# A graph kernel in which the counts of edges are built for 16 targets at a time instead of 32

## The chip, the cores and the metric

One Trainium2 chip, one of its cores. The metric is the device time of one execution in microseconds; the lower the better.

## The reference

1024 nodes with 128 features, 32768 edges sorted by their target, 64 features an edge. Two graph layers are computed:

```python
h = maximum(layernorm(x), 0)                       # [1024, 128]
m = mlp3(concat(h[src], h[dst], edge_attr))        # 320 -> 256 -> 256 -> 128, per edge
summed = segment_sum(m, src) + segment_sum(m, dst) # [1024, 128]
x = x + mlp3(concat(h, summed, attention(h)))      # attention: differences of paired blocks of 32 nodes
h = maximum(layernorm(x), 0)
deg = 1 + number of edges with this target
out = segment_sum over edges and self loops of dinv[src] * dinv[dst] * (h @ W)[src]  + b,  dinv = 1/sqrt(deg)
x = x + gelu(out)
```

The second layer needs, for every pair of nodes, how many edges lead from one to the other. The kernel builds this 1024 x 1024 table of counts while the edges of the first layer pass, and multiplies with it at the end.

## The kernel before, in words

**Head.** Layer norm, transposes, and two tables in DRAM (`table_a`, `table_b`) that hold each node's share of the first edge layer for source and target. GpSimd gathers rows of them by indirect DMA, 8 gathers for a group of 4 tiles of 128 edges (L446, L454), 64 groups in all, three buffers. VectorE prepares the edge indices, finds for each window of targets the first tile in which it occurs (L1156 to L1179) and writes it to `rows_i` (L1202).

**The loop over groups.** Each engine has a list of its own for group g, run by `run_groups`, unrolled:

- TensorE (`group`, L677): second layer of g (L607, 12 products of 512 columns), first layer of g+1 (L587, 4 products, then 8 transposes L593 that add the gathered rows), the scatter of tile 0 of g-1 between the two halves of that first layer, messages of g (L617), the scatter of tiles 1 to 3 of g-1 (L628). The count products (L646) stand one behind each of five transposes.
- ScalarE (`group`, L827): rounds the edges (L825), relu of both layers (L796, L802), the distance of each node's number to the middle of an edge's two ends (L812), rounds the messages (L819), and after every second group copies a window of counts out of PSUM (L853).
- VectorE (`group`, L1008): in this order one-hots of the next window (two pairs), incidence row 1 of g-1 (L1005), the sum of the gathered rows of g+1 (L1048, two halves), a pair of one-hots, incidence 2, low part of the edges of g+2 (L979), low part of the first layer (L985), incidence 3, one-hots, the other low part, one-hots, incidence 0 of g, low part of the messages (L991), and after every second group the sums of a window (L1076, L1078).

**The counts.** The sorted edges are cut into 32 windows of 32 targets. A window gets 10 tiles of edges, which covers what it spans. For each tile VectorE writes `oh_low` (128 x 128: which of 128 low source numbers) and `oh_key` (128 x 258, three rows of 86 padded to 88: which target and upper source number, 32 x 8 keys), and TensorE multiplies the two into `bank[2]`. Ten such products make the window (5 in each group). ScalarE copies it into `ct_sb`; VectorE sums it over sources (`into_part`) and targets (`from_part`). Where a window spans more than its tiles, a loop of extra visits adds the rest (`more_windows`); it runs at least once. With these inputs it runs once, both at 10 tiles for 32 targets and at 6 tiles for 16 targets. It stands behind group 62 on VectorE and in group 63 on TensorE. Then come the degrees (L664, L1145) and the bias of the messages times the number of edges (L1151).

**The end.** After the scatter of the last group TensorE adds that bias by 8 transposes (L672), ScalarE and VectorE copy the halves of the sums, and the update network (L714, L720, L728), the second layer norm, the product with the counts (L765), `gcn_W` (L744) and gelu follow.

## Time and profile before

| | us |
|---|---|
| median of 3 runs | 767.13 (765.44 to 767.53) |
| the profiled execution | 765.72 |
| its span | 763.9 |
| TensorE busy | 736.0 (96%) |
| VectorE busy | 729.5 (96%) |
| GpSimd busy | 539.0 (71%) |
| ScalarE busy | 524.3 (69%) |

The rows further down are times in us from the start of the span. A timeline row is: start, duration, engine and line, operation, output <- input with shapes, number of instructions merged; in brackets the idle time of the engine before it and what ended it. Ends of matmuls are modelled, and neighbouring instructions of an engine overlap somewhat, so the distance from start to start is what one costs in a row of them.

### The profile page before, as it was taken

How to read it: one execution, taken by the hardware profiler on the slowest of the kernel's cores; microseconds unless marked ns; L12 is line 12 of the kernel's file. 1: busy time of each engine (PE TensorE's matmuls, PEld its weight loads, DVE VectorE, ACT ScalarE, POOL GpSimd, SP SyncE). 2: the span in 40 equal slices, each digit the busy share in tenths (PEclk: the TensorE clock that was granted, in tenths of full speed). 3: DMA queues.
4: the chain of work that ended last, by engine and by line, in shares of the span. 5: the costliest groups of instructions: out<-in, count | busy, mean ns of one | idle time of the engine just before them, and what ended most of it. 6: DMA issues, size and time to landing. Idle time of an engine off the chain costs nothing.

```text
span 763.9 us, 13342 instructions
## 1 busy us (share of the span) xinstructions
PE 736.0 (96%) x4171; PEld 619.3 (81%) x4171; DVE 729.5 (96%) x1506; ACT 524.3 (69%) x711; POOL 539.0 (71%) x533
## 2 busy tenths in 40 slices
PE   7589999999999999999999999999999999999896
PEld 6467888888888888888888888888888888888755
DVE  7889999999999999999999999999999999999775
ACT  3256777777777777777777777777777777776623
POOL 3777777777777777777777777777777777777100
PEclk9899999999999999999999999999999999999999
DMA  7534444344434444344443444434443444432000
GB/s 227 164 119 129 128 127 123 117 126 129 126 112 125 130 128 127 114 124 128 127 124 113 130 129 126 126 112 127 129 126 113 126 127 130 126 111 83 0 1 28
DMA packets 42566, 90.15 MB, mean 118 GB/s; under 512 B 11136, under 2 KB 17920, under 8 KB 42496
## 3 DMA queue, kind: packets, MB, share of 16 engines
q0 software_dynamic: 24576, 67.14, 28.6%
q1 hardware_dynamic: 17920, 22.16, 9.9%
q8 instruction: 33, 0.54, 0.3%
q14 instruction: 37, 0.30, 0.1%
HBM read 86.64 MB, written 2.62 MB: 117 GB/s over the span
## 4 chain that ended last, share of the span: by engine, by line
PE 88%; DVE 4%; POOL 3%; issue 2%; DMA 2%; ACT 1%; DVEq 0%; SPq 0%; POOLq 0%
PE bank L628 30%; PE bank L607 22%; PE bank L617 14%; PE bank L587 7%; PE bank L593 7%; PE bank L646 4%; POOL rows_sb L446 2%; POOL rows_sb L454 1%; DVE ring L1005 1%; PE bank L720 1%; DMA w_sb<-mW 1%; PE bank L765 1%; PE bank L728 1%; DMA table_a<-rows_sb 0%; PE bank L714 0%
## 5 line engine op out<-in xcount | busy, mean ns | idle before, releaser
L446 POOL DMA_INDIRECT rows_sb<-table_a,ends_i x256 | 263.5, 1029 | 82.2 <-issue 77.7
L454 POOL DMA_INDIRECT rows_sb<-table_b,ends_i x256 | 262.7, 1026 | 78.0 <-issue 78.0
L812 ACT ACTIVATE dist<-iota_h,neg_mid 128x1026 f16<-128x1026 f16 (+1 forms) x256 | 292.3, 1143 | 0.0
L1005 DVE TENSOR_SCALAR ring<-dist,half_gap,times 128x1026 fp32r<-128x1026 f16 (+1 forms) x256 | 276.4, 1081 | 1.7 <-ACT dist L812 0.6
L628 PE MATMUL bank<-ring,m_hi 128*128 128x512 f32 x512 | 172.4, 418 | 1.3 <-DVE ring L1005 1.1
L802 ACT ACTIVATE h_sb<-bank,b_sb 128x512 f32<-128x512 f32 x128 | 87.6, 684 | 122.5 <-PE bank L607 122.5
L628 PE MATMUL bank<-ring,m_lo 128*128 128x512 f32 x512 | 160.8, 395 | 0.0
L607 PE MATMUL bank<-ring,w_hi 128*128 128x512 f32 x512 | 150.0, 394 | 1.4 <-DVE ring L985 1.4
L1057 DVE TENSOR_SCALAR oh_key<-iota_h,key_f,minus_base 128x258 bf16<-128x258 f16 x321 | 128.5, 400 | 0.0
L617 PE MATMUL bank<-w_sb,h_sb 128*128 128x128 f32 x1024 | 124.8, 275 | 0.0
L593 PE MATMUL bank<-ident,rows_sb 128*128 128x128 f32 x512 | 113.7, 276 | 8.0 <-DVE rows_sb L1048 8.0
L617 PEld LDWEIGHTS bank<-w_sb,h_sb 128*128 128x128 f32 x1024 | 119.5, 192 | 0.1
L796 ACT ACTIVATE ring<-bank 128x512 fp32r<-128x512 f32 x128 | 76.7, 599 | 60.1 <-PE bank L593 55.8
L607 PEld LDWEIGHTS bank<-ring,w_hi 128*128 128x128 f32 x512 | 96.1, 188 | 24.4 <-DVE ring L985 2.0
L628 PEld LDWEIGHTS bank<-ring,m_lo 128*128 128x128 f32 x512 | 96.9, 189 | 23.2
L628 PEld LDWEIGHTS bank<-ring,m_hi 128*128 128x128 f32 x512 | 87.2, 191 | 13.9 <-DVE ring L1005 2.0
L985 DVE SCALAR_TENSOR_TENSOR ring<-bank,ring 128x512 fp32r<-128x512 f32 x128 | 87.8, 686 | 3.7 <-ACT ring L796 1.7
L593 PEld LDWEIGHTS bank<-ident,rows_sb 128*128 128x128 f32 x512 | 70.3, 142 | 20.7 <-DVE rows_sb L1048 11.2
L1056 DVE TENSOR_SCALAR oh_low<-iota_h,low_f 128x128 bf16<-128x128 f16 x321 | 84.8, 264 | 2.2 <-issue 2.1
L1048 DVE TENSOR_TENSOR rows_sb<-rows_sb 128x512 f32<-128x512 f32 x128 | 82.2, 681 | 3.7 <-DMA rows_sb<-table_b,ends_i 3.6
L607 PE MATMUL bank<-ring,w_lo 128*128 128x512 f32 x256 | 80.3, 395 | 0.0
L646 PE MATMUL bank<-oh_key,oh_low 128*128 128x258 bf16 x320 | 77.8, 275 | 0.0
(182 smaller groups left out, 628.5 us busy)
## 6 DMA issues: line engine op xcount, KB each, us to landing
e_raw<-edge_attr_t SPq DMA_DIRECT2D x128, 128.0 KB, 3.1
rows_sb<-table_a,ends_i POOLq DMA_INDIRECT x256, 2.8
rows_sb<-table_b,ends_i POOLq DMA_INDIRECT x256, 2.9
table_a<-rows_sb SPq DMA_DIRECT2D x4, 256.0 KB, 3.4
table_b<-rows_sb SPq DMA_DIRECT2D x4, 256.0 KB, 2.5
x_sb<-x SPq DMA_DIRECT2D x2, 256.0 KB, 3.2
out<-oh_key SPq DMA_DIRECT2D x4, 128.0 KB, 1.8
u_sb<-uW SPq DMA_DIRECT2D x1, 384.0 KB, 5.0
```

The costliest lines, as they stand in the source:

```text
L446: nc.gpsimd.indirect_dma_start(got[:, b, t, 0, :], None, table_a, bass.IndirectOffsetOnAxis(ap=ends_i[:, 0, tile:tile + 1], axis=0),).then ...
L454: nc.gpsimd.indirect_dma_start(got[:, b, t, 1, :], None, table_b, bass.IndirectOffsetOnAxis(ap=ends_i[:, 1, tile:tile + 1], axis=0),).then ...
L593: mm = nc.tensor.matmul(z1t_bank[k][:, t * P:(t + 1) * P], got[:, g % GB, t, 0, part], ident[:, :], start=False, stop=True, is_transpose=T ...
L607: mm = nc.tensor.matmul(z2_bank[m][:, :], w[:, k, m * P:(m + 1) * P], a[:, b, k, :], start=(n == 0), stop=(n == len(parts) - 1))
L617: mm = nc.tensor.matmul(msg_bank[:, t * D:(t + 1) * D], h2_sb[:, k, t * P:(t + 1) * P], w3_sb[:, k, :], start=(t == 0 and k == 0), stop=(k ...
L628: mm = nc.tensor.matmul(acc_bank[n][:, :], part[:, b, t, :], inc[:, t, n * HB:(n + 1) * HB], start=(is_first(g) and t == 0 and part is m_h ...
L646: mm = nc.tensor.matmul(bank[2][:, 0:KR * KN], oh_low[:, w % HOT, j, :], oh_key[:, w % HOT, j, :, 0:KN], start=(j == 0), stop=(j == VT - 1 ...
L802: nc.scalar.activation(h2_sb[:, m, :], z2_bank[m][:, :], ACT.Relu, bias=b2_sb[:, m:m + 1]).then_inc(h2_ready, 1)
L812: nc.scalar.activation(to, of, ACT.Abs, bias=neg_mid[:, bass.ds(g * GT + t, 1)]).then_inc(dist_ready, 1)
L985: nc.vector.scalar_tensor_tensor(h1_lo[:, b, k, :], z1t_bank[k][:, :], 0.0, h1_hi[:, b, k, :].bitcast(F32), ALU.max, ALU.subtract).then_in ...
L1005: nc.vector.tensor_scalar(to, of, half_gap[:, tile], times[:, tile], ALU.is_equal, ALU.mult).then_inc(inc_ready, 1)
L1057: return nc.vector.tensor_scalar(oh_key[:, slot, j, :, 0:KN], iota_h[:, 0:KR * KN].rearrange("p (r n) -> p r n", r=KR), key_f[:, bass.ds(t ...
```

## The change

- A window is 16 targets wide instead of 32, there are 64 instead of 32, each gets 6 tiles instead of 10. `oh_key` is 128 columns, flat, without padding. One-hots have four buffers instead of two. VectorE makes two windows in each of the groups -1, 0 and 1, and one in each of the groups 2 to 59; window 0 is no longer built before the loop.
- TensorE counts a whole window (6 products in a row) between the first layer of g+1 and the messages of g, no longer one product behind a transpose. Two windows share a half of `bank[2]`.
- ScalarE clears `ct_sb` in the head with 8 activations of scale 0 (six after its table copies, two after its copies of the node part), and no longer copies windows. VectorE adds each pair of windows to `ct_sb` out of PSUM (`pair_out`), waits for that add, and sums as before, once for a pair.
- The extra visits are made ahead of the loop, behind the clears, and no longer touch the sums. `iota_f` moves to the memory of `dist`, since `ct_sb` is cleared.
- The degrees come one group earlier. The bias is added before the scatter of the last group, and that scatter does first all of the first 512 nodes and then the others (`last_scatter`).

```diff
-    VT = 10
-    NW = 32
+    VT = 6
+    NW = 64
     WD = N // NW
     WK = WD * NC
-    KR, KN, KP = 3, 86, 88
+    PAIRS = NW // 2
+    PD = 2 * WD
+    PK = 2 * WK
...
-    HOT = 2
+    HOT = 4
...
-        oh_key = sb("oh_key", [P, HOT, VT, KR, KP], BF16)
+        oh_key = sb("oh_key", [P, HOT, VT, WK], BF16)
...
-        from_part = sb("from_part", [P, NW, NC])
-        add_into = sb("add_into", [P, WD])
-        add_from = sb("add_from", [P, NC])
+        from_part = sb("from_part", [P, PAIRS, NC])
...
-        iota_f = ct_sb[:, 0, :]
+        iota_f = dist[:, :, :].rearrange("p t n -> p (t n)").bitcast(F32)[:, 0:N]
...
-        LAST_W = 2 * (NW - 1)
-
-        def made_in(i):
-
-            return 0 <= i and i + 1 < NW
-
-        def summed_in(b, i):
-
-            return b == 0 and 0 <= i < NW
+        FILL = 2
+
+        def made_in(g):
+
+            if g < FILL:
+                return [2 * (g + 1), 2 * (g + 1) + 1]
+            return [w for w in (g + 2 + FILL,) if w < NW]
+
+        def counted_in(g):
+
+            if 0 <= g <= FILL:
+                return [2 * g, 2 * g + 1]
+            return [w for w in (g + 1 + FILL,) if FILL < g and w < NW]
+
+        def summed_in(g):
+
+            pairs = [p for p in range(PAIRS) if 2 * p + 1 in counted_in(g - 1)]
+            return pairs[0] if pairs else None
+
+        LAST_SUM = NW - 1 - FILL
...
-            def first_layer(g, b, n, k, counting):
+            def first_layer(g, b, n, k):
...
-                    if counting and t in COUNTS_AT[k]:
-                        count_tile(counting[0], counting[1] * (VT // 2) + t - COUNTS_AT[k][0] + k * len(COUNTS_AT[0]))
...
-                return (w, (g + 1) % 2) if 0 <= w < NW else None
-
-            def count_tile(w, j):
-
-                if j % (VT // 2) == 0:
-                    pe.wait_ge(w_hot, 2 * w + j // (VT // 2) + 1)
-                if j == 0:
-                    wait(pe, w_out, w)
-                mm = nc.tensor.matmul(bank[2][:, 0:KR * KN], oh_low[:, w % HOT, j, :], oh_key[:, w % HOT, j, :, 0:KN],
-                                      start=(j == 0), stop=(j == VT - 1), skip_group_check=True)
-                if j == VT - 1:
-                    mm.then_inc(w_psum, 1)
+            def count_window(w):
+
+                pe.wait_ge(w_hot, w + 1)
+                if w % 2 == 0:
+                    wait(pe, w_out, w // 2 - 1)
+                at = (w // 2) % 2 * PK + w % 2 * WK
+                for j in range(VT):
+                    mm = nc.tensor.matmul(bank[2][:, at:at + WK], oh_low[:, w % HOT, j, :], oh_key[:, w % HOT, j, :],
+                                          start=(j == 0), stop=(j == VT - 1), skip_group_check=True)
+                mm.then_inc(w_psum, 1)
...
-                pe.wait_ge(w_out, NW)
                 visits = pe.value_load(rows_i[0:1, 2 * NW - 1:2 * NW], min_val=1, max_val=MORE)
                 with pe.Fori(0, visits) as v:
                     pe.wait_ge(more_hot, v + 1)
-                    nc.tensor.matmul(bank[2][:, 0:KR * KN], oh_low[:, 0, 0, :], oh_key[:, 0, 0, :, 0:KN],
+                    nc.tensor.matmul(bank[2][:, 0:WK], oh_low[:, 0, 0, :], oh_key[:, 0, 0, :],
                                      start=True, stop=True, skip_group_check=True).then_inc(more_psum, 1)
...
-                    mm = nc.tensor.matmul(acc_bank[c // 4][:, (c % 4) * P:(c % 4 + 1) * P], cb3[:, c, :], ident[:, :],
-                                          start=False, stop=(c % 4 == 3), is_transpose=True, skip_group_check=True)
-                    if c % 4 == 3:
-                        mm.then_inc(sums_ready, 1)
+                    nc.tensor.matmul(acc_bank[c // 4][:, (c % 4) * P:(c % 4 + 1) * P], cb3[:, c, :], ident[:, :],
+                                     start=False, stop=False, is_transpose=True, skip_group_check=True)
+
+            def last_scatter(g, b):
+
+                pe.wait_ge(m_lo_ready, g + 1)
+                for n in range(NH):
+                    for t in range(GT):
+                        if n == 0:
+                            pe.wait_ge(inc_ready, GT * g + (t + 1))
+                        for part in (m_hi, m_lo):
+                            mm = nc.tensor.matmul(acc_bank[n][:, :], part[:, b, t, :], inc[:, t, n * HB:(n + 1) * HB],
+                                                  start=False, stop=(t == GT - 1 and part is m_lo),
+                                                  skip_group_check=True)
+                    mm.then_inc(sums_ready, 1)
             def group(g, b, i):
                 now, nxt, past = exists(g), exists(g + 1), exists(g - 1)
+                if g == GROUPS:
+                    add_bias_of_sums()
+                    last_scatter(g - 1, 1 - b)
+                    return
...
-                if g == LAST_W + 1:
-                    more_windows()
                 if nxt:
-                    first_layer(g + 1, 1 - b, i + b, 0, counts_of(g))
+                    first_layer(g + 1, 1 - b, i + b, 0)
                 if past:
                     scatter(g - 1, 1 - b, 0)
                 if nxt:
-                    first_layer(g + 1, 1 - b, i + b, 1, counts_of(g))
+                    first_layer(g + 1, 1 - b, i + b, 1)
+                for w in counted_in(g):
+                    count_window(w)
                 if now:
                     messages(g)
-                if g == LAST_W + 1:
+                if g == LAST_SUM + 1:
                     count_ends()
                 if past:
                     scatter(g - 1, 1 - b, 1)
@@ -701,11 +718,10 @@
             turn_starts()
             pe.wait_ge(uh_ready, KH * NH)
             pe.wait_ge(w_lo_ready, 4)
+            pe.wait_ge(rows_ready, 1)
+            more_windows()
             pe.wait_ge(w1e_lo_ready, 1)
-
-            pe.wait_ge(rows_ready, 1)
             run_groups(pe, group, FIRST + 1)
-            add_bias_of_sums()
...
+            def clear_counts(chunks):
+
+                for c in chunks:
+                    nc.scalar.activation(ct_sb[:, c, :], iota_h[:, 0:N], ACT.Copy, scale=0.0).then_inc(ct_zero, 1)
+
+            act.wait_ge(dve_step, 2)
+            clear_counts(range(0, NC - 2))
...
-                if summed_in(b, i):
-                    window_out(i)
-
-            def window_out(w):
-
-                act.wait_ge(w_psum, w + 1)
-                nc.scalar.copy(ct_sb[:, :, bass.ds(w * WD, WD)],
-                               bank[2][:, 0:WK].rearrange("p (d a) -> p a d", a=NC)).then_inc(w_out, 1)
...
                                      bias=ub1_sb[:, m:m + 1]).then_inc(uh_ready, 1)
+            clear_counts(range(NC - 2, NC))
             nc.scalar.copy(w1e_hi[:, :], w1e_sb[:, :]).then_inc(w1e_hi_ready, 1)
...
-                makes = made_in(i)
-                if makes:
-                    tile0 = window_tile(i + 1)
-                    one_hots(i + 1, tile0, b, (0, 1))
+                makes = made_in(g)
+                steady = makes and g >= FILL
+                if steady:
+                    w = makes[0]
+                    tile0 = window_tile(w)
+                    one_hots(w, tile0, (0, 1))
                 if past:
                     incidence(g - 1, 1)
                 if nxt:
...
-                if makes:
-                    one_hots(i + 1, tile0, b, (2,))
+                if steady:
+                    one_hots(w, tile0, (2,))
...
-                if makes:
-                    one_hots(i + 1, tile0, b, (3,))
+                if steady:
+                    one_hots(w, tile0, (3,))
                 if nxt:
                     low_first(g + 1, 1 - b, 1)
-                if makes:
-                    one_hots(i + 1, tile0, b, (4,))
+                if steady:
+                    one_hots(w, tile0, (4, 5))
                 if now:
                     incidence(g, 0)
                     low_messages(g, b)
-                if summed_in(b, i):
-                    window_sums(i)
+                if not steady:
+                    for w in makes:
+                        one_hots(w, window_tile(w), range(VT))
+                pair = summed_in(g)
+                if pair is not None:
+                    pair_out(pair)
...
-                return nc.vector.tensor_scalar(oh_key[:, slot, j, :, 0:KN],
-                                               iota_h[:, 0:KR * KN].rearrange("p (r n) -> p r n", r=KR), key_f[:, bass.ds(tile, 1)], base,
+                return nc.vector.tensor_scalar(oh_key[:, slot, j, :], iota_h[:, 0:WK], key_f[:, bass.ds(tile, 1)], base,
...
-            def one_hots(w, tile0, half, tiles):
+            def one_hots(w, tile0, tiles):
                 if tiles[0] == 0:
-                    wait(dve, w_psum, w - 1)
+                    wait(dve, w_psum, w - HOT + 1)
                 base = minus_base[:, bass.ds(w, 1)]
-                for t in tiles:
-                    j = half * (VT // 2) + t
+                for j in tiles:
                     hot = one_hot(w % HOT, j, tile0 + j, base)
-                    if t == VT // 2 - 1:
+                    if j == VT - 1:
                         hot.then_inc(w_hot, 1)
...
-            def window_sums(w):
-
-                dve.wait_ge(w_out, w + 1)
-                counts = ct_sb[:, :, bass.ds(w * WD, WD)]
-                nc.vector.tensor_reduce(into_part[:, bass.ds(w * WD, WD)], counts.rearrange("p a d -> p d a"),
+            def pair_out(p):
+
+                dve.wait_ge(w_psum, 2 * p + 2)
+                counts = ct_sb[:, :, bass.ds(p * PD, PD)]
+                found = bank[2][:, p % 2 * PK:(p % 2 + 1) * PK].rearrange("p (d a) -> p a d", a=NC)
+                nc.vector.tensor_tensor(counts, counts, found, ALU.add).then_inc(w_out, 1)
+                dve.wait_ge(w_out, p + 1)
+                nc.vector.tensor_reduce(into_part[:, bass.ds(p * PD, PD)], counts.rearrange("p a d -> p d a"),
                                         AX_X, ALU.add)
-                nc.vector.tensor_reduce(from_part[:, bass.ds(w, 1), :].rearrange("p w a -> p (w a)"), counts,
+                nc.vector.tensor_reduce(from_part[:, bass.ds(p, 1), :].rearrange("p w a -> p (w a)"), counts,
                                         AX_X, ALU.add).then_inc(w_sums, 1)
             def more_windows():
-                dve.wait_ge(w_sums, NW)
+                dve.wait_ge(ct_zero, NC)
...
-                STEPS = 15
+                STEPS = 11
...
                     dve.wait_ge(more_psum, v + 1)
-                    then(nc.vector.tensor_reduce(add_into[:, :], counts.rearrange("p (d a) -> p d a", a=NC),
-                                                 AX_X, ALU.add))
-                    then(nc.vector.tensor_reduce(add_from[:, :], counts.rearrange("p (d a) -> p a d", a=NC),
-                                                 AX_X, ALU.add))
                     to = ct_sb[:, :, bass.ds(w * WD, WD)]
                     then(nc.vector.tensor_tensor(to, to, counts.rearrange("p (d a) -> p a d", a=NC), ALU.add))
                     dve.wait_ge(more_step, v * STEPS + done[0])
-                    to = into_part[:, bass.ds(w * WD, WD)]
-                    then(nc.vector.tensor_tensor(to, to, add_into[:, :], ALU.add))
-                    to = from_part[:, bass.ds(w, 1), :].rearrange("p w a -> p (w a)")
-                    then(nc.vector.tensor_tensor(to, to, add_from[:, :], ALU.add))
-                    dve.wait_ge(more_step, v * STEPS + done[0])
                 assert done[0] == STEPS
+
+            def sum_counts():
+
+                dve.wait_ge(w_sums, PAIRS)
                 nc.vector.tensor_reduce(deg_out[:, :], from_part[:, :, :].rearrange("p w a -> p a w"),
                                         AX_X, ALU.add).then_inc(into_ready, 1)
...
+            more_windows()
             dve.wait_ge(w1e_hi_ready, 1)
...
             low_edges(0, 0)
-            tile0 = window_tile(0)
-            for half in range(2):
-                one_hots(0, tile0, half, range(VT // 2))
-
-            run_groups(dve, group, FIRST + 1, {1: count_passes, LAST_W: more_windows, LAST_W + 1: degrees})
+            run_groups(dve, group, FIRST + 1, {1: count_passes, LAST_SUM: sum_counts, LAST_SUM + 1: degrees})
```

## Rows read from the trace of the kernel before

**Rows 1.** Busy us (count) by engine in VectorE's groups 2-59; clock; DMA; GB/s

```profile
62.27:680.50 618.23, 617.85 (x3533) 525.75 (x3532) 613.54 (x1218) 455.61 (x609) 476.87 (x465) 1.00 0.41 124
```

**Rows 2.** Timeline of TensorE: start, us, line, operation, count

```profile
300.14 0.27 PE L593 MATMUL bank<-ident,rows_sb 128*128 128x128 f32 x1
300.25 0.27 PE L646 MATMUL bank<-oh_key,oh_low 128*128 128x258 bf16 x1
...
309.87 0.39 PE L587 MATMUL bank<-e_parts,w1e_hi 128*128 128x512 f32 x1
...
320.55 0.39 PE L587 MATMUL bank<-e_parts,w1e_hi 128*128 128x512 f32 x1
```

**Rows 3.** Timeline of VectorE in the loop, two groups

```profile
299.36 0.24 DVE L1056 TENSOR_SCALAR oh_low<-iota_h,low_f 128x128 bf16<-128x128 f16 x1
...
303.39 0.25 DVE L1056 TENSOR_SCALAR oh_low<-iota_h,low_f 128x128 bf16<-128x128 f16 x1
303.55 0.40 DVE L1057 TENSOR_SCALAR oh_key<-iota_h,key_f,minus_base 128x258 bf16<-128x258 f16 x1
303.87 0.68 DVE L985 SCALAR_TENSOR_TENSOR ring<-bank,ring 128x512 fp32r<-128x512 f32 x1
...
306.80 0.60 DVE L1076 TENSOR_REDUCE into_part<-ct_sb 128x32 f32<-128x256 f32 x1
307.32 0.40 DVE L1078 TENSOR_REDUCE from_part<-ct_sb 128x8 f32<-128x256 f32 x1
307.64 0.42 DVE L1056 TENSOR_SCALAR oh_low<-iota_h,low_f 128x128 bf16<-128x128 f16 x1
...
308.60 0.81 DVE L1005 TENSOR_SCALAR ring<-dist,half_gap,times 128x1024 fp32r<-128x1024 f16 x1
309.32 1.28 DVE L1048 TENSOR_TENSOR rows_sb<-rows_sb 128x512 f32<-128x512 f32 x2
310.52 0.25 DVE L1056 TENSOR_SCALAR oh_low<-iota_h,low_f 128x128 bf16<-128x128 f16 x1
...
320.70 0.24 DVE L1056 TENSOR_SCALAR oh_low<-iota_h,low_f 128x128 bf16<-128x128 f16 x1
```

**Rows 4.** Timeline of GpSimd in the loop, two gathers in a row

```profile
309.83 1.59 POOL L446 DMA_INDIRECT rows_sb<-table_a,ends_i  x1 [0.30 <-issue]
311.72 0.94 POOL L454 DMA_INDIRECT rows_sb<-table_b,ends_i  x1 [0.30 <-issue]
```

**Rows 5.** Waits of VectorE: waited for, us in total, times, longest us

```profile
DVE rows_sb L1048 <- DMA rows_sb<-table_b,ends_i: 3.6, 2, 2.9
...
DVE ring L985 <- ACT ring L796: 1.7, 2, 0.9
```

**Rows 6.** Timeline of TensorE at the end; idle time before in brackets

```profile
684.20 0.27 PE L593 MATMUL bank<-ident,rows_sb 128*128 128x128 f32 x1
...
705.54 0.33 PE L593 MATMUL bank<-ident,rows_sb 128*128 128x128 f32 x1
...
717.68 0.28 PE L657 MATMUL bank<-oh_key,oh_low 128*128 128x258 bf16 x1 [2.03 <-DVE oh_key L1057]
...
727.80 0.74 PE L628 MATMUL bank<-ring,m_hi 128*128 128x512 f32 x2 [1.14 <-DVE ring L1005]
...
732.30 1.98 PE L714 MATMUL bank<-rows_sb,u_sb 128*128 128x512 f32 x4 [0.24 <-ACT rows_sb L870]
```

**Rows 7.** Timeline of VectorE in the visit at the end

```profile
714.16 0.23 DVE L1096 TENSOR_SCALAR over_f<-rows_f,visit_f 1x32 f32<-1x32 f32 x1 [1.19 <-issue]
...
718.67 0.41 DVE L1120 TENSOR_TENSOR ct_sb<-ct_sb,bank 128x256 f32 x1
```

**Rows 8.** Timeline of VectorE in the head

```profile
26.86 0.18 DVE L1202 CAST rows_i<-rows_f 1x64 int32<-1x64 f32 x1
```

**Rows 9.** Timeline of ScalarE in the head

```profile
26.35 0.69 ACT L861 ACTIVATE uh_sb<-bank,ub_sb 128x512 f32<-128x512 f32 x1 [0.76 <-PE bank L571]
```

**Rows 10.** Timeline of ScalarE at the end, distance instructions

```profile
716.48 2.18 ACT L812 ACTIVATE dist<-iota_h,neg_mid 128x1024 f16<-128x1024 f16 x2
```

6 lines of the change are left out of this document (2 added, 4 removed).

## The prediction, made before the changed kernel was run

> **What bounds the kernel now.** I first read the busy time by stretch. From the second group of edges to the sixtieth both TensorE and VectorE are busy practically all the time, at full clock (granted clock 1.00, the 2.4 GHz level): 617.9 and 613.5 of 618.2 us for 58 groups, so a group takes 10.66 us, and ScalarE has slack [rows 1]. "Busy" can hide waiting, so the timelines are read next, taking from one start to the next start, since neighbouring instructions overlap by about 0.08 us.
>
> TensorE: the first product of a group's first layer, L587, starts at 309.87 and at 320.55, 10.68 apart, and the timeline between them has no gap. One transpose and one count product take 0.11 us each [rows 2]. So TensorE paces the loop, with work of 10.66 us of which the 5 count products are 0.55; without them it would need 10.11.
>
> VectorE alternates: the group with the window sums takes 11.16 us, the one without 10.18 [rows 3]. Its work: a one-hot pair 0.48 (oh_low 0.16, oh_key 0.32), the two sums 0.52 + 0.32 = 0.84. 10.18 - 5 x 0.48 = 7.78 is everything else. The group with sums should then take 11.02, so it waits about 0.12 once in two groups. VectorE's own work averages 10.60 us a group, only 0.06 us (0.6%) less than TensorE's. That is the fact that decides this change: anything added to VectorE in the loop beyond 0.06 us a group is paid in full.
>
> GpSimd has 8 gathers a group, 1.026 us busy on average [rows 1] and 0.30 between them: 10.6, also the pace of the loop, but with stretched gathers (1.59 beside 0.94) [rows 4]; undisturbed, 8 x 1.25 = 10.0.
>
> The head, up to the start of VectorE's group 2 at 62.27, is set by gathers and then by VectorE, which waits 3.6 us for two of them [rows 5]. At the end TensorE sits idle for 2.03 us before the product of the visit at 717.68, and starts the update network at 732.30 [rows 6].
>
> **VectorE in the loop.** A group now builds 6 pairs of 128 + 128 columns instead of 5 of 128 + 258. oh_low stays 0.16. oh_key has two pointer scalars: 258 elements took 0.32 and the incidence row of 1024 elements, the same kind of instruction, 0.72 [rows 3]; the slope is 0.52 ns an element and the fixed part 0.185. So 128 elements cost 0.25 at that slope and 0.185 if the elements were free; with oh_low's 0.16 (one pointer) as the outermost bound. I take 0.22, the middle of 0.185 and 0.25, because the new operand is flat like oh_low's and no longer in three padded rows. A pair: 0.38. Six: 2.28, against 2.40: -0.12 a group.
>
> The window's copy leaves ScalarE (no gain: it has slack) and becomes an add on VectorE, once in two groups: 0.41 for this shape in the visit [rows 7], 0.33 after the overlap. The sums wait for this add's own semaphore, so the overlap is lost and a short gap comes: +0.12 (bounds 0 to 0.2). Behind that waiting instruction stand the sums and the next group's one-hots and incidence rows, and TensorE waits for the latter. Add and sums: 0.45 + 0.52 + 0.33 = 1.30, against 0.84: +0.23 a group.
>
> Together 7.78 + 2.28 + 0.65 = 10.71 us a group, against the present pace of 10.66. With oh_key at 0.185: 10.50; at 0.25: 10.89.
>
> **TensorE in the loop.** 6 products of 128 columns in a row, instead of 5 of 258 between transposes. A product of half the columns costs 0.055 if the columns count and 0.11 if loading 128 weights does [rows 2]; I take 0.07, nearer the columns: 0.42 a group. 10.11 + 0.42 = 10.53 (10.44 to 10.77). So the pace passes from TensorE to VectorE, and TensorE's saving of 0.13 a group buys nothing.
>
> **The whole stretch on VectorE**, from the converted window rows (27.04 [rows 8]) to the start of group 60 (680.5 before [rows 1]):
> - The visit must wait for 8 clears by ScalarE. Six lie in a stretch in which ScalarE is idle; two stand behind the last copy of the node part, which ends at 27.04 [rows 9]. A clear is like a distance instruction, two of which take 2.18 [rows 10]: VectorE waits until 29.15, +2.1 (0 to 2.3). It is queued ahead of the low edges of group 0, for which TensorE waits.
> - The visit itself: 1.19 us of register loads, then 714.16 to 719.08, less the two reductions that go (0.67), and 0.2 to its end [rows 7]: +5.65. Before, VectorE built window 0 here, while gathers landed.
> - One-hot pairs: 384 x 0.38 = 145.9, against 310 x 0.48 = 148.8 (ten come later): -2.9. All 64 windows are built by group 59, 12 pairs a group in the first three.
> - Sums: 31 x 1.30 = 40.3 against 30 x 0.84 = 25.2: +15.1.
> - Waiting that the added work fills: 3.6 for gathers and 1.7 for the first-layer halves [rows 5], 0.7 before the first one-hots and the low edges, 29 x 0.12 in the loop: 9.5; about 1.5 remains in the first group: -8.0.
> Sum: +12.0; group 60 begins at 692.5.
>
> **The end.** Groups 60 to 63 have no one-hots, so VectorE needs 7.8 to 9 us and TensorE leads again. Its transposes of group 61 began at 684.20, 3.7 us after VectorE's group 60; now they follow the pair sums at once, at 692.5 + 0.72 + 0.6 + 0.1 = 693.9: +9.7. From there to the update network it took 732.30 - 684.20 = 48.10 [rows 6]. After: 10.53 and 10.11 for two groups. From the transposes of group 63 (705.54 before) the pieces are: first layer and one scatter 1.90, messages 1.70, degree columns 1.75, scatter 2.88, second layer 2.79, scatter 0.93, messages 1.79, scatter 2.88, bias 0.95, last scatter 3.75: 21.3. Sum 41.9: -6.2. What goes: the visit's stall (2.8 with its product), the counts (1.2), a wait of 1.1 for a late incidence row behind the degrees, and the copy after the bias (0.6), which the second half of the scatter now covers. After it the kernel is as before.
>
> Result: +12.0 - 2.3 (the lag of TensorE behind VectorE that vanishes) - 6.2 = +3.5 us. The profiled execution took 765.72 us (span 763.9); 769.2 by its own time, and 770.6 against the median of 767.13, 0.5% slower.
>
> **Rivals.** (A) Faster: the flat oh_key is as cheap as oh_low. It decides from 0.19 down. Then a VectorE group is 7.78 + 1.92 + 0.65 = 10.35, under TensorE's 10.53, which paces on; group 2 begins 2.2 us earlier, the transposes of group 61 at 680.4, 3.8 before today's, and the end gains its 6.2: -10.0, 757. Against it: the fixed part of the two-pointer kind, 0.185, is alone above oh_low's whole 0.16 [rows 3]. The Trainium skill, VectorE: DVE Perf Modes, section "The TRN2 errata", gives 58 cycles and a quarter of a cycle an element, 0.094 us for such an instruction; by it the group would be 9.96 and the result this rival's 757. Here oh_low took 0.16, so the trace does not agree, and I hold to the rows.
>
> (B) Slower by TensorE: the six products in a row cost 0.11 each. A group is 10.77, over VectorE's 10.71: 58 x 0.06 = 3.5, 774. For it: the weights change at each product. Against it: the 258 columns of today's count product already cost 0.11 by themselves at this clock, so nothing shows that the weights cost as much; no row here has a run of 128-column products of this type.
>
> (C) Slower by GpSimd: gathers fall behind. They start the loop 7.7 us ahead of VectorE compared with now, since they aren't delayed in the head; they decide from a group of 10.71 + 7.7/58 = 10.84. Gathers stretch when VectorE's work falls on them: 0.94 to 1.59 [rows 4], in all 0.6 us a group. If the 6 flat oh_key add half of that again and more, a group reaches 11.0: 58 x 0.29 - 7.7 = +9, 780. The Trainium skill, SBUF - State Buffer, section "Who interferes with whom", says that a tensor_scalar in a two-port mode and GpSimd lock each other out; by it each flat one-hot is a further lock. The stretched gathers of rows 4 agree with such a lock.
>
> (D) The change does less than it says in the loop, but its ends count: waiting for the own add costs nothing and a clear is short: -0.12 x 31 and -1.5: 765 to 766. No second visit arises: the longest of the 64 windows spans 6 tiles, which is what is built.
>
> **Chances.** Forecast 0.45 (766 to 775), A 0.2, B 0.1, C 0.1, D 0.15. The range is 756 to 780: it leaves out some of A and half of C. What this kernel's measurement can tell from no change is about 0.3%, 2.3 us. Faster takes A and half of D: 0.27; same the rest of D and the low part of the forecast: 0.23; slower 0.50.
>
> **What would show it.** VectorE's oh_key at 0.28 to 0.32 duration (0.22 start to start); two groups of VectorE at 10.07 and 11.36; TensorE idle 0.1 to 0.2 us a group before the transposes of L593, with the pair sums L1048 named as releaser; the first product of group 0 near 36 us; the second layer of group 0 near 40.2; VectorE's group 2 at 70; no stall at the end. I am wrong if TensorE still has no gap in the loop (A or B), or if VectorE waits for gathers there (C).

## The result, and the profile after

The changed kernel takes 785.23 us (783.21 to 788.11) against 767.11 us (765.44 to 767.53) before: a ratio of 1.0242, 95% interval 1.0212 to 1.0272. It is 18.1 us slower. The forecast was 770.6 us with a range of 756 to 780; the direction was right, the size wrong, and the range too narrow. The profiled execution took 783.60 us (span 781.9), 17.9 more than the profiled one of before; all sums below are made against it. The four executions of the changed kernel lie 4.9 us apart, so a difference of 2 to 3 us between its median and that of a variant says little by itself. Where such a difference matters, the traces are compared stretch by stretch; variants in which the loop was not edited need 618.5 to 618.8 us from the low messages of group 2 to those of group 59, the changed kernel 619.5, so about 1 us over the loop is chance too.

First the split at three points that the prediction had named: the start of VectorE's group 2, that of its group 60, and the first product of the update network (VectorE's groups start behind the window or pair sums).

| stretch | before | forecast | after | after against forecast |
|---|---|---|---|---|
| head, to group 2 | 62.27 | 70.0 | 73.71 | +3.7 |
| loop, 58 groups | 618.2 | 622.5 | 630.9 | +8.4 |
| end, group 60 to the update network | 51.8 | 43.3 | 45.7 | +2.4 |
| from the start to the update network | 732.3 | 735.8 | 750.3 | +14.5 |

The loop in the changed kernel, as in [rows 1] (columns: window, length, busy us and count on PE, PEld, DVE, ACT, POOL, granted clock, DMA share, GB/s), and a stretch of the head:

```profile
73.71:704.61 630.90, 620.21 (x3594) 518.08 (x3595) 626.17 (x1367) 439.18 (x578) 488.91 (x466) 1.00 0.41 122
40.00:60.00 20.00, 14.26 (x73) 11.63 (x74) 18.57 (x61) 9.08 (x14) 15.73 (x15) 0.84 0.38 119
```

TensorE is no longer full: 10.7 us idle in the loop, where [rows 1] had 0.4, and what it waits for is the pair adds, as the bracket names them (idle us before the row, and who ended it):

```profile
316.73 0.44 PE L605 MATMUL bank<-ident,rows_sb 128*128 128x128 f32 x2 [0.16 <-DVE rows_sb L1070]
```

VectorE is full, and paces. That is the handover that the prediction forecast, at a worse rate: 630.9 / 58 = 10.88 us a group, not 622.5 / 58 = 10.73. The timeline of VectorE, columns as in [rows 3], from the low messages of one group on; the last two rows stand in the group behind it:

```profile
311.96 0.68 DVE L1007 TENSOR_TENSOR m_lo<-bank,m_hi 128x512 fp32r<-128x512 f32 x1
312.56 0.41 DVE L1097 TENSOR_TENSOR ct_sb<-ct_sb,bank 128x256 f32<-128x256 f32 x1
313.00 0.62 DVE L1099 TENSOR_REDUCE into_part<-ct_sb 128x32 f32<-128x256 f32 x1
313.54 0.41 DVE L1101 TENSOR_REDUCE from_part<-ct_sb 128x8 f32<-128x256 f32 x1
313.86 0.28 DVE L1078 TENSOR_SCALAR oh_low<-iota_h,low_f 128x128 bf16<-128x128 f16 x1
314.06 0.30 DVE L1079 TENSOR_SCALAR oh_key<-iota_h,key_f,minus_base 128x128 bf16<-128x128 f16 x1
314.28 0.24 DVE L1078 TENSOR_SCALAR oh_low<-iota_h,low_f 128x128 bf16<-128x128 f16 x1
...
315.39 1.28 DVE L1070 TENSOR_TENSOR rows_sb<-rows_sb 128x512 f32<-128x512 f32 x2
...
319.67 0.84 DVE L1021 TENSOR_SCALAR ring<-dist,half_gap,times 128x1024 fp32r<-128x1024 f16 x1
320.43 0.24 DVE L1078 TENSOR_SCALAR oh_low<-iota_h,low_f 128x128 bf16<-128x128 f16 x1
...
329.84 0.89 DVE L1021 TENSOR_SCALAR ring<-dist,half_gap,times 128x1024 fp32r<-128x1024 f16 x1
330.65 0.24 DVE L1078 TENSOR_SCALAR oh_low<-iota_h,low_f 128x128 bf16<-128x128 f16 x1
```

Read from start to start: the pair's add 0.44 (312.56 to 313.00, forecast 0.45), the sums 0.54 and 0.32, oh_key 0.22 (314.06 to 314.28, forecast 0.22). But the flat incidence row of 1024 elements, 0.72 in [rows 3], takes 0.76 at 319.67 and 0.81 at 329.84, and oh_low behind the sums 0.20 instead of 0.16. This is the rule and not an exception: over groups 3 to 58 the 112 such rows average 0.766, where the kernel before has 0.724, and the 28 oh_low behind sums average 0.209, before 0.159. What lies beside these rows on GpSimd, in the changed kernel:

```profile
315.17 2.33 POOL L458 DMA_INDIRECT rows_sb<-table_a,ends_i  x1 [0.30 <-issue]
...
319.05 0.95 POOL L458 DMA_INDIRECT rows_sb<-table_a,ends_i  x1 [0.30 <-issue]
...
329.27 0.95 POOL L458 DMA_INDIRECT rows_sb<-table_a,ends_i  x1 [0.30 <-issue]
```

The gather at 319.05 ends at 320.00, 0.33 us after the incidence row began; the one at 329.27 ends 0.38 after. A row of the kernel before that takes 0.73 (the next instruction starts at 319.50), and its gather, which ends 0.29 after the row's start:

```profile
318.77 0.81 DVE L1005 TENSOR_SCALAR ring<-dist,half_gap,times 128x1024 fp32r<-128x1024 f16 x1
```
```profile
318.11 0.95 POOL L446 DMA_INDIRECT rows_sb<-table_a,ends_i  x1 [0.30 <-issue]
```

So in the changed kernel the rows are longer the later the running gather ends: 0.72 where it ends up to 0.20 us after the row's start, 0.76 to 0.77 at 0.29 to 0.34, 0.80 to 0.82 at 0.37 and 0.38. The end of the gather isn't all of it, since the kernel before has rows of 0.72 to 0.74 at 0.29 to 0.31, where the changed kernel has 0.76; what makes that difference isn't known. The other way round, the gather at 315.17, which began 0.22 us before the pair adds and while an incidence row still ran, took 2.33 us instead of 0.95. (Another, at 325.40, also began just before a pair of adds and in an incidence row, and took 1.06; what makes a gather that long isn't settled.) The two engines hold each other up. The prediction had looked at one direction alone (rival C: VectorE stretches the gathers). The Trainium skill, SBUF — State Buffer, section "Who interferes with whom", has both, for VectorE instructions in a two-port mode: whoever issues first gets the shared ports for the whole instruction, and the other blocks fully. The rows agree in kind and not in size: a row that overlaps its gather by 0.33 or 0.38 us pays 0.04 or 0.09.

### The profile page after: what moved, and what is told of

It reads as the page before. It is cut to its first block, busy times and chain, and to the rows that moved or that the text cites. A ratio compares the mean times of both kernels' runs of the same rounds, so it can differ in the third digit from the quotient of the medians.

```text
span 781.9 us, 13729 instructions
## 1 busy us (share of the span) xinstructions
PE 740.4 (95%) x4235; PEld 614.3 (79%) x4235; DVE 744.0 (95%) x1662; ACT 516.4 (66%) x687; POOL 549.6 (70%) x533
## 4 chain that ended last, share of the span: by engine, by line
DVE 63%; issue 18%; PE 12%; DVEq 5%; ACT 1%; POOL 0%; POOLq 0%
DVE ring L1021 16%; DVE rows_sb L1070 10%; DVE oh_key L1079 9%; DVE ring L1001 7%; DVE oh_low L1078 6%; DVE e_parts L995 5%; DVE m_lo L1007 4%; PE bank L638 2%; DVEq L1075 1%; PE bank L627 1%; DVEq L1079 1%; PE bank L617 1%; DVE ct_sb L1097 1%; DVE into_part L1099 1%; DVEq L1078 1%
## 5 line engine op out<-in xcount | busy, mean ns | idle before, releaser
L458 POOL DMA_INDIRECT rows_sb<-table_a,ends_i x256 | 270.7, 1057 | 82.9 <-issue 77.7
L466 POOL DMA_INDIRECT rows_sb<-table_b,ends_i x256 | 265.9, 1039 | 78.0 <-issue 78.0
L638 PE MATMUL bank<-ring,m_hi 128*128 128x512 f32 x504 | 170.3, 419 | 0.0
L627 PE MATMUL bank<-w_sb,h_sb 128*128 128x128 f32 x1024 | 128.2, 278 | 0.1
L1079 DVE TENSOR_SCALAR oh_key<-iota_h,key_f,minus_base 128x128 bf16<-128x128 f16 x385 | 127.6, 333 | 0.0
L605 PE MATMUL bank<-ident,rows_sb 128*128 128x128 f32 x512 | 87.1, 285 | 18.3 <-DVE rows_sb L1070 15.6
L605 PEld LDWEIGHTS bank<-ident,rows_sb 128*128 128x128 f32 x512 | 62.3, 143 | 52.4 <-DVE rows_sb L1070 38.6
L1078 DVE TENSOR_SCALAR oh_low<-iota_h,low_f 128x128 bf16<-128x128 f16 x385 | 95.4, 248 | 2.4 <-issue 2.2
L1070 DVE TENSOR_TENSOR rows_sb<-rows_sb 128x512 f32<-128x512 f32 x128 | 86.6, 715 | 0.0
L617 PEld LDWEIGHTS bank<-ring,w_lo 128*128 128x128 f32 x256 | 48.7, 190 | 10.8
```

The costliest lines, as they stand in the source:

```text
L458: nc.gpsimd.indirect_dma_start(got[:, b, t, 0, :], None, table_a, bass.IndirectOffsetOnAxis(ap=ends_i[:, 0, tile:tile + 1], axis=0),).then ...
L466: nc.gpsimd.indirect_dma_start(got[:, b, t, 1, :], None, table_b, bass.IndirectOffsetOnAxis(ap=ends_i[:, 1, tile:tile + 1], axis=0),).then ...
L605: mm = nc.tensor.matmul(z1t_bank[k][:, t * P:(t + 1) * P], got[:, g % GB, t, 0, part], ident[:, :], start=False, stop=True, is_transpose=T ...
L617: mm = nc.tensor.matmul(z2_bank[m][:, :], w[:, k, m * P:(m + 1) * P], a[:, b, k, :], start=(n == 0), stop=(n == len(parts) - 1))
L627: mm = nc.tensor.matmul(msg_bank[:, t * D:(t + 1) * D], h2_sb[:, k, t * P:(t + 1) * P], w3_sb[:, k, :], start=(t == 0 and k == 0), stop=(k ...
L638: mm = nc.tensor.matmul(acc_bank[n][:, :], part[:, b, t, :], inc[:, t, n * HB:(n + 1) * HB], start=(is_first(g) and t == 0 and part is m_h ...
```

## The experiments

The diffs are against the changed kernel, or against the kernel before where the text says so.

**Take the gathers away.** In the changed kernel (the last 30 groups then work on rows that were gathered earlier, so the output is not the true one; one execution was taken):

```diff
+        GATHERED = 34
...
-            for g in range(1, GROUPS):
+            for g in range(1, GATHERED):
...
-                        dve.wait_ge(ga_done[b][t], 16 * (n + 1))
-                        dve.wait_ge(gb_done[b][t], 16 * (n + 1))
+                        if g < GATHERED:
+                            dve.wait_ge(ga_done[b][t], 16 * (n + 1))
+                            dve.wait_ge(gb_done[b][t], 16 * (n + 1))
```

> The changed kernel, in which the gathers of groups 34 to 63 are left out (their sums are taken of rows gathered before). Theory (VectorE and GpSimd hold each other up): up to group 33 VectorE's two groups take 10.22 and 11.49 us as in the changed kernel; from there on the flat incidence rows take 0.72 from start to start instead of 0.76 to 0.81 and the first one-hot behind the sums 0.16 instead of 0.21, so the groups take 10.08 to 10.12 and 11.34 to 11.38, 10.71 to 10.75 on average, as was predicted for the change. With 27 such groups and no sum of GpSimd beside the pair adds at the end: 777 to 780 us. Rival (the excess of 0.13 to 0.15 a group is VectorE's own, or TensorE's): the groups stay at 10.22 and 11.49, and only the end gains: 782 to 784.

Measured 783.85 us. VectorE just behind the last gather, and in a later group (columns as before):

```profile
389.10 3.19 DVE L1080 TENSOR_SCALAR oh_low<-iota_h,low_f 128x128 bf16<-128x128 f16 x1
...
505.22 0.81 DVE L1022 TENSOR_SCALAR ring<-dist,half_gap,times 128x1024 fp32r<-128x1024 f16 x1
```

The flat row at 505.22 is back at 0.72 from start to start, and from group 34 on the groups average 10.11 without sums and 11.44 with them, where the changed kernel has 10.22 and 11.49. From group 33 to group 59, by the low messages, 26 groups take 280.06 us, against 282.17: 0.08 us a group, over 58 groups 4.7 of the 8.4 us. So the theory holds, and the rival (the excess is VectorE's or TensorE's own) fails for most of the excess.

The excess can be counted out in the changed kernel's own trace. Averaged over groups 3 to 58, from start to start, a group takes 10.86: the two flat incidence rows are 0.09 over twice 0.72, the oh_low behind the sums adds 0.02, and a pair of one-hots costs 0.385 and not 0.38, which makes 0.03 in six. That is the 0.14 over the forecast of 10.71. The first two go with the gathers (the rows fall to 0.722 on average, most of those oh_low to 0.16), and 0.02 of this gain are taken back by stray one-hots that last 0.1 to 0.2 us longer; the third is a rounding of the forecast.

The total did not move because the row at 389.10 gives it back: an oh_low that took 3.19 us beside GpSimd's sum for x_sb, which now came in the middle of the loop and began 0.70 us after the oh_low:

```profile
389.80 2.42 POOL L487 TENSOR_TENSOR x_sb<-x_sb,ub_all 128x1024 f32<-128x1024 f32 x1
```

At the end of the changed kernel this same sum blocks the pair adds (3.81 us at 713.19) and costs nothing, since VectorE would have waited for ScalarE behind them: here, with the sum gone from that place, it waits 2.26 us at 716.97 for a distance instead. So my expectation of 777 to 780 us, with a gain at the end, was wrong.

**The same in the kernel before** (again one execution).

> The kernel before, in which the gathers of groups 34 to 63 are left out in the same way. Theory (there TensorE sets the pace, and the gathers are no bound): the groups stay at 10.66 to 10.68 us, VectorE's still alternate between about 10.30 and 11.02 with the small wait, and the time is 763 to 767 us (the adds of GpSimd at the end start earlier or later, no more). Rival (GpSimd sets the pace before, TensorE only seems full): a group falls to 10.60 or less from group 34 on, and the time to 762 or less.

Measured 766.36 us. The same 26 groups take 276.84 us, 10.65 each, against 277.36 (10.67) with gathers, and the wait of 0.1 before the first low_first half stays. The 0.5 us are VectorE catching up after the same stall by GpSimd's sum: for four pairs of groups it runs at 11.02 and 10.17 to 10.18, 10.60 on average, and then falls back to 11.02 and 10.31. TensorE did pace the loop before; GpSimd did not.

**The add itself.** ScalarE copies the pair, as it copied the windows before; what the visit found is overwritten:

```diff
-                nc.vector.tensor_tensor(counts, counts, found, ALU.add).then_inc(w_out, 1)
...
+            def pair_copy(p):
+                act.wait_ge(w_psum, 2 * p + 2)
+                nc.scalar.copy(ct_sb[:, :, bass.ds(p * PD, PD)],
+                               bank[2][:, p % 2 * PK:(p % 2 + 1) * PK].rearrange("p (d a) -> p a d", a=NC)).then_inc(w_out, 1)
```

> The changed kernel, in which ScalarE copies the counts of a pair out of PSUM again, instead of VectorE's add onto the cleared counts; the clears and the visit at the head stay, and what the visit found is overwritten (that part of the computation is left out). Theory (VectorE paces the loop, and its pair add with its own wait costs 0.44 us in two groups): the group with sums falls from 11.49 to 11.05, the average from 10.86 to 10.63, 58 x 0.22 = 12.9 less, as far as TensorE's 10.4 to 10.5 allows: 772 to 775 us. Rival (the gathers pace the loop through their stretching): a group stays above 10.8, 782 to 785.

Measured 768.87 us, ratio to the kernel before 1.0032 (1.0015 to 1.0050): 16.4 us come back by the medians, 13.3 by the profiled executions (770.35). From the low messages of group 2 to those of group 59 it is 14.6 us (604.85 against 619.49), more than the 12.9 expected: the group with sums falls from 11.49 to 10.98, not 11.05, and the average to 10.59. VectorE, once in two groups:

```profile
305.79 0.68 DVE L1016 TENSOR_TENSOR m_lo<-bank,m_hi 128x512 fp32r<-128x512 f32 x1
306.39 0.59 DVE L1105 TENSOR_REDUCE into_part<-ct_sb 128x32 f32<-128x256 f32 x1
306.90 0.40 DVE L1107 TENSOR_REDUCE from_part<-ct_sb 128x8 f32<-128x256 f32 x1
307.23 0.24 DVE L1087 TENSOR_SCALAR oh_low<-iota_h,low_f 128x128 bf16<-128x128 f16 x1
```

The add of 0.44 is gone, and the 0.05 of the oh_low behind the sums with it. So the one part that the prediction priced at 0.23 us a group (13.5 us in all) is the largest part of the change's loss: taking it away gives 0.26 a group back. What is left, by the traces against the kernel before, is a head that is 10.3 us longer up to the low messages of group 2, a loop that is 3.1 us shorter and an end that is 2.5 us shorter. The rival (gathers pace the loop) falls for the changed kernel, but not for this one. At its end:

```profile
701.19 0.69 DVE L1079 TENSOR_TENSOR rows_sb<-rows_sb 128x512 f32<-128x512 f32 x1 [2.87 <-DMA rows_sb<-table_b,ends_i]
```
```profile
715.14 0.44 PE L605 MATMUL bank<-ident,rows_sb 128*128 128x128 f32 x2 [3.11 <-DVE rows_sb L1079]
```

VectorE waits 2.87 us for a gathered row. By the first gather of a group, groups 10 to 57 start 10.735 us apart on GpSimd, VectorE's 10.59: the lead of the gathers melts away, GpSimd's own sums then fall on an incidence row ahead of the pair adds (4.99 us at 709.24 instead of 0.81), and TensorE waits 3.11.

**The layout of the keys.** oh_key in 4 rows of 32, padded to 34 (what else names `oh_key` is adapted):

```diff
+    KR, KN, KP = 4, 32, 34
...
-        oh_key = sb("oh_key", [P, HOT, VT, WK], BF16)
+        oh_key = sb("oh_key", [P, HOT, VT, KR, KP], BF16)
```

> The changed kernel with oh_key laid out in 4 rows of 32 columns, padded to 34, as the kernel before had 3 rows of 86. Theory (the layout does not matter for the contention, and each row costs at most a little): oh_key 0.22 to 0.26 from start to start instead of 0.22, the flat incidence rows still 0.76 to 0.81, so 785 to 799 us. Rival (the flat one-hots are what hold the gathers up and are held up by them): the incidence rows go back to 0.72, no gather takes 2.33 us any more, and the time falls by 5 to 8 us, to 777 to 780.

Measured 784.97 us, ratio 1.0246 (1.0224 to 1.0269), the changed kernel's. Groups of instructions between 320 and 640 us (columns: line, engine, operation, tiles, shapes, count; busy us, mean ns; idle before):

```profile
L1080 DVE TENSOR_SCALAR oh_key<-iota_h,key_f,minus_base 128x128 bf16<-128x128 f16 x179 | 59.6, 333 | 0.0
L1022 DVE TENSOR_SCALAR ring<-dist,half_gap,times 128x1024 fp32r<-128x1024 f16 x59 | 49.9, 845 | 0.0
```

333 and 845 ns, 333 and 848 in the changed kernel: four rows of 32 in place of one of 128 cost nothing and buy nothing. (Three rows, as in the kernel before, weren't run at 128 columns. For the incidence rows three pieces do cost: 1026 elements take 1.25 to 1.36 us from start to start, 1024 flat ones 0.72.) The prediction had taken 0.22 "because the new operand is flat"; the value was right, the reason not. Rival A rested on the same idea. The Trainium skill, VectorE: DVE Perf Modes, section "The TRN2 errata", would have an estimated 0.094 us for it by its row `58 + FD/Accel`; here it took 0.22 in either layout.

**The head: order or clock.** TensorE in the head of the changed kernel (idle time before in brackets):

```profile
36.20 0.77 PE L599 MATMUL bank<-e_parts,w1e_hi 128*128 128x512 f32 x1 [1.95 <-DVE e_parts L995]
...
58.66 0.44 PE L605 MATMUL bank<-ident,rows_sb 128*128 128x128 f32 x2 [4.21 <-DVE rows_sb L1070]
...
75.95 0.44 PE L605 MATMUL bank<-ident,rows_sb 128*128 128x128 f32 x2 [4.28 <-DVE rows_sb L1070]
```

The first product came at 36.20 as forecast (near 36), and the visit began at 30.37 and ended near 34.8, as the sum had it. The lateness arises behind it: TensorE waits 4.21 and 4.28 us for the pair adds, which stand behind 12 pairs of one-hots. The mean granted clock of 0.84 is made of stretches at the lower level of 1.2 GHz (0.50); in the changed kernel, columns as in [rows 1]:

```profile
41.50:45.80 4.30, 4.30 (x11) 3.34 (x12) 4.30 (x23) 0.69 (x1) 3.15 (x4) 0.50 0.31 100
59.50:62.80 3.30, 3.30 (x16) 2.74 (x15) 3.07 (x4) 2.01 (x3) 2.64 (x3) 0.50 0.34 101
76.60:79.80 3.20, 3.20 (x12) 2.65 (x13) 3.14 (x6) 1.63 (x2) 2.47 (x3) 0.50 0.29 87
```

The second and the third follow the two waits. The first lies ahead of both, behind the 7 us in which TensorE waits for the visit, and its end moves from one execution to the next: with the same head, the run without gathers is at 1.00 from 41.50 to 45.80. Two kernels are meant to tell the order from the clock. One builds windows 1, 3 and 5 a group later, behind the pair adds:

```diff
+                if 0 <= g <= FILL:
+                    one_hots(2 * g + 1, window_tile(2 * g + 1), range(VT))
...
-                    for w in makes:
+                    for w in makes[0:1]:
                         one_hots(w, window_tile(w), range(VT))
```

> The changed kernel, in which windows 1, 3 and 5 are built one group later, behind that group's pair adds, so that 6 pairs of one-hots stand ahead of the pair adds of groups 1 and 2, not 12. Theory (in the head TensorE waits for the pair adds, 4.2 and 4.3 us at 54.3 and 71.5, and works at the lower clock after each wait): each wait is 2 to 2.3 us shorter, VectorE's third group starts 2.5 to 4.5 us earlier than 73.7, and the time is 781 to 783 us. Rival (VectorE's own work sets the head, and TensorE only follows): the third group starts within 0.5 us of 73.7, and the time stays at 785.

Measured 782.60 us, ratio 1.0209 (1.0194 to 1.0225). TensorE:

```profile
55.67 0.44 PE L605 MATMUL bank<-ident,rows_sb 128*128 128x128 f32 x2 [1.89 <-DVE rows_sb L1077]
...
69.94 0.44 PE L605 MATMUL bank<-ident,rows_sb 128*128 128x128 f32 x2 [1.26 <-DVE rows_sb L1077]
```

The waits are 1.89 and 1.26. The low messages of group 2 come at 80.33 instead of 83.22. The profiled execution (784.74) lost this again at its end, in the same way as above: from the low messages of group 59 to the update network it takes 52.63 us, the changed kernel 47.62.

```profile
713.15 0.69 DVE L1077 TENSOR_TENSOR rows_sb<-rows_sb 128x512 f32<-128x512 f32 x1 [2.90 <-DMA rows_sb<-table_b,ends_i]
```

The other fills TensorE's waits with products that nobody reads:

```diff
+            keep_busy(40)
             more_windows()
+            keep_busy(10)
...
+                if g == 1:
+                    pe.wait_ge(m_lo_ready, 1)
+                    for _ in range(20):
+                        nc.tensor.matmul(msg_bank[:, 0:P], ident[:, :], ident[:, :], start=True, stop=True)
```

(and the same 20 products at g == 0, without the wait)

> The changed kernel with products that nobody reads in three of TensorE's waits in the head: 50 around the visit, 20 ahead of the first layers of groups 1 and 2. Theory (the lower clock after these waits costs TensorE's half-speed products on the path to the next pair adds): the granted clock between 40 and 80 us goes from 0.84 to 0.9 or more, the third group of VectorE starts 2 to 4 us earlier than 73.7, the time is 781 to 783 us. Rival (VectorE's own work sets the head): the clock rises, the third group starts within 0.5 us of 73.7, the time stays at 785. If the added products stand in the way themselves, it is slower by up to 3 us.

Measured 786.54 us, ratio 1.0268 (1.0248 to 1.0289).

```profile
40.00:60.00 20.00, 18.43 (x141) 16.92 (x140) 15.86 (x56) 9.55 (x14) 15.21 (x16) 1.00 0.46 141
```

The clock is at the full 1.00 (the 2.4 GHz level) between 40 and 60 us, but 0.92 between 60 and 80: in place of two stretches of 3.4 us at the lower level there is one of 6.8, from 76.7 on. By the low messages:

| from | changed kernel | spread windows | filled waits |
|---|---|---|---|
| group 0 to 1 | 14.40 | 12.88 | 12.96 |
| group 1 to 2 | 17.39 | 16.55 | 17.99 |
| together | 31.78 | 29.43 | 30.94 |

So the order is worth 2.35 us, and that is shown: two other runs with the changed kernel's head take 32.11 and 31.63 for the two groups together, and 14.72 and 14.25 for the first. How much of it is the clock is not: in the first of the two groups the full clock alone, with the order left as it was, gives nearly as much (1.44) as the new order (1.52), and in the second it was not kept up. The start of this stretch came 3.3 us later by the added products, so as a whole the kernel with them was no faster. Both the theory's 781 to 783 us and the rival's unchanged start of group 2 missed; the added products stood in the way themselves, as the expectation's last sentence allows.

**The visit at the head**, left out; the wait for the clears moved to the first pair's add:

```diff
-            more_windows()
...
+                if p == 0:
+                    dve.wait_ge(ct_zero, NC)
```

> The changed kernel with the visit at the head left out (on this data it finds nothing, so only its work goes), and the wait for the cleared counts moved to the first pair's add. Theory: the head of the change costs what VectorE does and waits there, 2.85 us for the clears and 4.3 for the visit, less what a gather wait gives back: VectorE's third group starts 4 to 6 us earlier than 73.7 and the time is 779 to 781 us. If the prediction's part sum was right in this term (7.75 put in, 5.5 of it covered by waits that were there before), the gain is only 2 to 3 us: 782 to 783. Rival (the head is lost to the double windows alone): nothing moves, 785.

Measured 781.67 us, ratio 1.0207 (1.0184 to 1.0231): 3.6 us less by the medians, 2.6 by the low messages of group 59 (700.08 against 702.71) and 1.9 by those of group 2 (81.34 against 83.22), behind which nothing was edited. I had expected 4 to 6 here; the prediction's own term (7.75 put in, 5.5 of it covered by waits that were there before) gives 2.3, and it was the better one. The rival (nothing moves) fails by the traces.

**The end.** GpSimd waits for the bias input before it adds the diagonal:

```diff
-            pool.wait_ge(into_ready, 1)
+            pool.wait_ge(cb3_ready, 1)
```

> The changed kernel, in which GpSimd adds the diagonal only once the bias products are formed on VectorE (some 12 us later), so not beside the pair adds of group 63. Theory: these take 1.28 us instead of 3.47, TensorE's waits of 0.80 and 0.42 us before the transposes of group 63 go, and the time is 1.2 us lower, 784.0. Rival (another wait takes its place, or the adds on GpSimd then stand in the way of the last incidence rows): 785 to 787.

Measured 782.44 us, ratio 1.0216 (1.0197 to 1.0235). In the changed kernel, VectorE, GpSimd and TensorE around the pair adds of group 63:

```profile
725.50 3.47 DVE L1070 TENSOR_TENSOR rows_sb<-rows_sb 128x512 f32<-128x512 f32 x2
```
```profile
724.94 2.61 POOL L491 TENSOR_TENSOR ct_sb<-ct_sb,ident 128x896 f32<-128x896 f32 x1 [9.10 <-DVE deg_out L1146]
```
```profile
728.16 0.44 PE L605 MATMUL bank<-ident,rows_sb 128*128 128x128 f32 x2 [0.80 <-DVE rows_sb L1070]
729.02 0.44 PE L605 MATMUL bank<-ident,rows_sb 128*128 128x128 f32 x2 [0.42 <-DVE rows_sb L1070]
```

The diagonal's 2.61 us start 0.56 before the adds, and these take 3.47. In the experiment:

```profile
725.21 1.28 DVE L1070 TENSOR_TENSOR rows_sb<-rows_sb 128x512 f32<-128x512 f32 x2
```
```profile
726.55 0.44 PE L605 MATMUL bank<-ident,rows_sb 128*128 128x128 f32 x2 [0.16 <-DVE rows_sb L1070]
```

1.28 again, and a wait of 0.16. From the first transposes of group 61 to those of group 63 it takes 20.85 us instead of 21.56 (forecast 20.64), and from there (725.95) to the update network 21.93 instead of 22.17 (forecast 21.3). From the low messages of group 59 on, 0.93 us are gained in all; the rest of the 2.8 between the medians lies ahead of this place, where nothing was edited, and isn't explained.

**The change's end alone, in the kernel before** (last_scatter as in the change, with the bias ahead of it):

```diff
+                if g == GROUPS:
+                    add_bias_of_sums()
+                    last_scatter(g - 1, 1 - b)
+                    return
...
             run_groups(pe, group, FIRST + 1)
-            add_bias_of_sums()
```

> The kernel before with the change's end alone: the bias products ahead of the last scatter, which is done half by half. Theory, as in the prediction: the copy of the first half of the sums hides behind the second half of the scatter, -0.6 us (766.2), and nothing else moves; the larger gains at the end (the visit's stall, 2.8 us) don't come from this part. Rival (the end of the change did nothing, or made it longer, and its gain of 4.6 us came from the visit alone): 766.8 to 767.5.

Measured 766.95 us, ratio 1.0002 (0.9993 to 1.0011): nothing, as the rival had it.

```profile
730.52 1.09 PE L672 MATMUL bank<-ident,cb 128*128 128x128 f32 x8 [1.46 <-DVE cb L1165]
```

The bias products now wait 1.46 us for their input, which VectorE forms behind the low messages of group 63, where the last scatter used to wait 1.14 for an incidence row [rows 6]. Whether the new order pays where the counts are ready a group earlier, as with the 64 windows, no run tells apart.

**Two attempts at a faster kernel.** The first combines what had helped: ScalarE's copy, no clears, the visit behind the pair adds of group 63, windows 0 and 1 ahead of the first pair adds, 3 and 5 behind later ones, the diagonal late.

```diff
-            more_windows()
             dve.wait_ge(w1e_hi_ready, 1)
...
             low_edges(0, 0)
+            one_hots(0, window_tile(0), range(VT))
+            one_hots(1, window_tile(1), range(VT))
...
                 if nxt:
                     add_pairs(g + 1)
+                if g == LAST_SUM + 1:
+                    more_windows()
+                    sum_counts()
```

> A combination: the 64 windows, the 128-column keys and the last scatter of the change, but ScalarE copies the pairs (no add on VectorE, no clears), the visit stands behind the pair adds of group 63 instead of at the head, windows 0 and 1 are built while the first gathers land, windows 3 and 5 behind pair adds, the degree products at the end of their group and the diagonal added late. Theory: VectorE's own groups average 10.59 as in the run with ScalarE's copy, GpSimd's gathers with their stretching some 10.6 to 10.7, so the loop is at best 4 us under the kernel before; the end is 4 to 5 us shorter than before, less 1 for the visit: 761 to 764 us. Rival (the gathers fall behind the pair adds, as they did at the end of the run with the spread windows, and take the gain of the loop back; the end still gains): 764 to 767.

Measured 769.53 us, ratio 1.0033 (1.0014 to 1.0053): 0.3% slower than the kernel before, so the theory (761 to 764) and the rival (764 to 767) both missed.

```profile
39.73 0.69 DVE L1084 TENSOR_TENSOR rows_sb<-rows_sb 128x512 f32<-128x512 f32 x1 [1.74 <-DMA rows_sb<-table_b,ends_i]
44.58 0.69 DVE L1084 TENSOR_TENSOR rows_sb<-rows_sb 128x512 f32<-128x512 f32 x1 [4.16 <-DMA rows_sb<-table_b,ends_i]
...
699.56 0.69 DVE L1084 TENSOR_TENSOR rows_sb<-rows_sb 128x512 f32<-128x512 f32 x1 [3.05 <-DMA rows_sb<-table_b,ends_i]
```

VectorE waits for gathers at both ends of the loop. The low messages of group 2 come at 79.39, before at 72.00: six windows have to be built by then. The loop gives back only 2.0 us (605.9 against 607.9 from group 2 to 59), and the end 0.7.

The second is the kernel before with the last scatter, the late diagonal, and the first scatter of group 62 ahead of the visit's product:

```diff
                 if past:
                     scatter(g - 1, 1 - b, 0)
+                if g == LAST_W + 1:
+                    more_windows()
```

> The kernel before with the change's last scatter, the diagonal added by GpSimd only behind the bias products' input, and the first scatter of group 62 ahead of the visit's product on TensorE. Theory: the four incidence rows that took 4.55 us beside GpSimd's adds take 3.3, so the low messages of group 63 and the degrees come 1.2 us earlier and TensorE's wait for the bias input (1.46 us with the last scatter alone) goes; the scatter of 1.1 us fills half of the visit's stall: 1.5 to 2.5 us less, 764.5 to 765.5. Rival (VectorE's chain behind the visit still ends last, the scatter moved ahead buys nothing): 0.5 to 1.2 us less, 765.8 to 766.4.

Measured 766.55 us, ratio 0.9994 (0.9985 to 1.0003): no difference that can be told, and less than even the rival's 0.5 us.

```profile
717.55 0.28 PE L657 MATMUL bank<-oh_key,oh_low 128*128 128x258 bf16 x1 [1.07 <-DVE oh_key L1071]
...
726.41 1.09 PE L672 MATMUL bank<-ident,cb 128*128 128x128 f32 x8 [1.33 <-DVE cb L1165]
...
729.67 0.50 PE L683 MATMUL bank<-ring,m_hi 128*128 128x512 f32 x1 [0.55 <-DVE ring L1019]
```

The stall before the visit's product shrinks from 2.03 [rows 6] to 1.07, as expected, and TensorE then waits 0.33 (at 720.26), 1.33 and 0.55 for VectorE. The chain behind the visit is VectorE's, so work moved on TensorE only moves its waits.

## Why the prediction was wrong, step by step

The mechanism was right and the sum too small in three places: VectorE's work beside the added pieces in the loop (7.78 us a group, measured 7.88, which with two smaller terms is 8.4 us of the 14.5), the waits left in the head (3.7) and the end (2.4).

- *VectorE becomes the bound*: right. The pace passed from TensorE to VectorE, with TensorE idle before the transposes, VectorE's pair sums named.
- *One-hot pair 0.38*: right to 0.005 (0.385 on average, which makes 0.03 a group in six), but not for the reason given: four rows cost the same as a flat operand.
- *Add and sums 1.30*: right within a row (0.44 + 0.54 + 0.32). What was missed is the 0.05 that the next one-hot pays beside a gather, 0.02 a group.
- *Everything else 7.78*: this is the term that failed in the loop. It was read from groups in which the gathers cost the flat incidence rows nothing, and taken as VectorE's own in any order of the work. It measured 7.88 on average, 0.09 of the 0.10 in the two incidence rows, and in the run without gathers the rows are back at 0.72. With the 0.02 behind the sums and the 0.03 of the pairs this makes the 0.14 by which a group came out too short, together +8.4 us.
- *TensorE 10.53 a group, 0.07 a count product*: too dear, by 0.08 in the six products, and it did not matter. Six products from 318.37 to the next product at 318.71 are 0.34 us, 0.057 each; rival B was never near:

```profile
318.37 0.50 PE L650 MATMUL bank<-oh_key,oh_low 128*128 128x128 bf16 x6
318.71 2.00 PE L627 MATMUL bank<-w_sb,h_sb 128*128 128x128 f32 x16
```

- *The head, visit and clears*: right to 0.1 us up to 34.8. *"About 1.5 remains in the first group"* failed: from the visit to group 2 VectorE waited 4.2 us (without 0.56 of register loads, which were there before). I had added up VectorE's work and let the waits fill, without following where the two early windows stand: ahead of the pair adds, so that TensorE waits, works at 1.2 GHz for 3.4 us after each wait, and hands its wait back to VectorE. +3.7, of which the order is 2.35 by the run with the spread windows; the clock's part of that isn't parted from it, and the rest isn't assigned.
- *The end, -6.2*: it gained 4.6 from group 63's transposes (22.17 against 26.76, forecast 21.3). The forecast had not asked what into_ready releases: with the counts ready a group earlier, GpSimd's diagonal adds move from beside incidence rows to beside the pair adds. That is 0.93 of the 2.4 us; the rest is 0.6 before the transposes of group 61 (1.99 us behind VectorE's group 60, forecast 1.4), and 0.8 that isn't assigned, 0.6 of it behind the transposes of group 63.
- *The copy hidden by the half scatter (0.6)*: not shown as a gain of its own; alone it brought nothing.
- *Rivals*: A had no ground (0.22, not 0.16), B neither. C named the right pair of engines and 780 us, but the gathers never fell behind in the changed kernel. They did at the end of the variant in which ScalarE copies, of the combination, and of the one with the spread windows, whose loop ran at the changed kernel's pace: there the last gather of a group ended 6.2 us ahead of the second pair add in group 8, and 2.1 in group 62 (in the changed kernel 12.6 and 13.2). C was given 0.1, and the range stopped at its price.
- *The range*: it was made of single terms, each with its bounds. Nearly all of the three errors lay in how the parts meet (a gather and a row, a burst and an add, a release and an add), and all pointed up. That VectorE would pace and the kernel be slower was well founded; that the pair of one-hots came out at 0.38 was partly luck.

## What to carry to other kernels

Where an engine has 0.6% of slack, price first what the change adds to it, and then ask of each added or moved piece what stands behind it and what runs beside it on the engine that it holds up and is held up by. An engine's "own" work read from a trace holds only for the phase in which the neighbour's instructions lay in that trace. And three engines within 1% of one another mean that relief of one brings the next: taking the add away gave 13 to 16 us back, and then the gathers stood in the way.

## What was not expected of the hardware

- In the changed kernel a flat incidence row of 1024 elements took 0.72 us with a gather ending up to 0.20 us after its start, 0.76 at 0.33 and 0.81 at 0.38. In the kernel before it took 0.72 to 0.74 up to 0.31. The rows of 1026 elements in three pieces took 1.25 to 1.36 with and without gathers.
- An oh_low of 128 elements that began 0.70 us before GpSimd's sum over 128 x 1024 floats (2.42 us) took 3.19 us instead of 0.24, and ended 0.07 us behind that sum.
- The lead of the gathers over the pair adds is not a constant: with VectorE at 10.59 us a group, GpSimd needed 10.735 for 8 gathers that took 10.656 in the kernel before; with VectorE at 10.85, 10.91 in the run with the late diagonal.
